# GNN layer with a ternary feed-forward: a second bank for the block sums, five feed-forward banks, smaller loads

## What is computed

```python
xn = layernorm(x)                                    # 6250 x 512
agg = segment_sum(xn[src], dst); neigh = agg / max(deg, 1)
h = layernorm(xn @ W_self + b_self + neigh @ W_neigh) * gamma + beta
x1 = x + where(h >= 0, h, alpha * h) + xn
z = layernorm(x1)
out = x1 + (silu(z @ Qg.T) * (z @ Qu.T)) @ Qd.T      # Q: ternary weights, one scale per 128 inputs
```

## Time and profile before

| | us |
|---|---|
| runs, median of 3 (lowest to highest) | 1532.24 (1531.26 to 1532.78) |
| the profiled execution | 1530.48 |
| its span, first to last instruction | 1528.0 |
| TensorE busy | 1477.2 (97%) |
| ScalarE busy | 1175.0 (77%) |
| VectorE busy | 1050.5 (69%) |
| GpSimd busy | 941.5 (62%) |

### The profile page before, as it was taken

How to read it: one execution, slowest core, us unless ns; L and a number is a source line. 1 busy time by engine, 2 the same in 40 slices (tenths; PEclk the granted TensorE clock), 3 DMA queues, 4 the chain that set the end, 5 groups by cost and what they waited for, 6 DMA issues and landing times.

```text
span 1528.0 us, 21758 instructions
## 1 busy us (share of the span) xinstructions
PE 1477.2 (97%) x6421; PEld 763.3 (50%) x6422; DVE 1050.5 (69%) x2305; ACT 1175.0 (77%) x2248; POOL 941.5 (62%) x936
## 2 busy tenths in 40 slices
PE   7899998998999999999999999999999998999897
PEld 3444444555555555555555555555555554554343
DVE  8999644566767676675675757667577675765876
ACT  5467720014888888889898897979989998998896
POOL 2113237776777777777777777777777777774000
PEclk9999999999999999999999999999999999999999
DMA  8978459999988888898888878888888888885101
GB/s 309 282 262 260 136 178 336 333 301 279 245 241 250 238 266 248 243 269 215 283 229 253 234 239 246 239 252 233 243 223 245 233 257 242 231 245 145 36 14 41
DMA packets 210386, 353.39 MB, mean 231 GB/s; under 512 B 104986, under 2 KB 104986, under 8 KB 210258
## 3 DMA queue, kind: packets, MB, share of 16 engines
q0 software_dynamic: 70560, 231.27, 52.0%
q1 hardware_dynamic: 139708, 120.73, 26.4%
HBM read 295.79 MB, written 39.62 MB: 220 GB/s over the span
## 4 chain that ended last, share of the span: by engine, by line
PE 84%; DMA 5%; DVE 3%; POOL 3%; issue 2%; SPq 1%; ACT 1%; POOLq 0%; DVEq 0%; ACTq 0%
PE f_ps L971 22%; PE f_ps L972 21%; PE f_ps L785 16%; PE agg_ps L867 11%; PE agg_ps L869 11%; POOL rows L737 3%; PE side_ps L912 1%; DMA x1T<-hsx 1%; DMA rows<-node_table,idx 1%; DMA node_table<-hsx 1%; DMA own_rows<-acc 1%; PE agg_ps L781 1%; DVE st6p L1140 1%; DMA xj<-xnt_rows 1%; PE side_ps L781 1%
## 5 line engine op out<-in xcount | busy, mean ns | idle before, releaser
L737 POOL DMA_INDIRECT rows<-node_table,idx x882 | 893.1, 1013 | 302.5 <-issue 266.0
L1065 ACT ACTIVATE f_ps<-f_ps,ratio 128x512 f32<-128x512 f32 (+2 forms) x1303 | 777.0, 674 | 120.4 <-PE f_ps L972 115.5
L971 PE MATMUL f_ps<-x1T,tern 128*128 128x512 f16 (+2 forms) x1144 | 415.5, 367 | 11.8 <-DMA x1T<-hsx 4.9
L972 PE MATMUL f_ps<-x1T,tern 128*128 128x512 f16 (+2 forms) x1144 | 415.3, 367 | 0.0
L867 PE MATMUL agg_ps<-rows,hot 128*128 128x512 f16 x846 | 323.0, 382 | 7.9 <-DMA rows<-node_table,idx 5.5
L869 PE MATMUL agg_ps<-rows,hot 128*128 128x512 f16 x846 | 320.6, 379 | 0.0
L1415 DVE SCALAR_TENSOR_TENSOR acc<-f_ps,scl,acc 128x512 f32<-128x512 f32 (+2 forms) x143 | 102.3, 716 | 176.5 <-PE f_ps L972 116.3
L971 PE MATMUL f_ps<-hT,tern 128*128 128x512 f16 (+2 forms) x572 | 208.5, 367 | 0.4 <-DVE acc L1415 0.2
L972 PE MATMUL f_ps<-hT,tern 128*128 128x512 f16 (+2 forms) x572 | 208.4, 367 | 0.0
L867 PEld LDWEIGHTS agg_ps<-rows,hot 128*128 128x128 f16 x846 | 119.4, 141 | 115.2 <-issue 35.2
L972 PEld LDWEIGHTS f_ps<-x1T,tern 128*128 128x128 f16 x1144 | 112.1, 98 | 124.7 <-issue 1.8
(11 more groups left out here) (174 smaller groups left out, 1698.9 us busy)
## 6 DMA issues: line engine op xcount, KB each, us to landing
rows<-node_table,idx POOLq DMA_INDIRECT x882
hsx<-own_rows SPq DMA_DIRECT2D x49, 256.0 KB
hsx<-in_x SPq DMA_DIRECT2D x48, 256.0 KB
out_nodes<-work SPq DMA_DIRECT2D x48, 256.0 KB, 3.8
node_table<-work SPq DMA_DIRECT2D x30, 256.0 KB, 2.3
xj<-xnt_rows SPq DMA_DIRECT2D x26, 256.0 KB, 4.5
acc<-own_rows SPq DMA_DIRECT2D x23, 256.0 KB, 4.8
own_rows<-acc SPq DMA_DIRECT2D x23, 256.0 KB, 5.8
```

The costliest lines, as they stand in the source:

```text
L737: pool.indirect_dma_start(out=rows[:, j, :], out_offset=None, in_=table[:, :], in_offset=bass.IndirectOffsetOnAxis(ap=of[:, j:j + 1], axis ...
L971: pe.matmul(to, lhs, parts[0], start=g == 0, stop=False, skip_group_check=True)
L972: pe.matmul(to, lhs, parts[1], start=False, stop=True, skip_group_check=True).then_inc(p_ff, 1)
L1065: act.activation(ps, ps, ACT.Copy, scale=ratio[:, w if up else 2, j:j + 1]).then_inc(a_scaled, 1)
```

## The change

It has six parts.

1. The sums of blocks alternate between `agg_ps` and a new bank `agg2_ps` at all blocks; `sum_step` waits for the read of the block before the last only.
2. `AGG_AT`: one sum step in each of the 18 ticks, in place of none in ticks 0 and 1 and two in ticks 2 and 10.
3. `LANES` 5 in place of 6; the planner gives another order. In the table stage `agg2_ps` is the sixth of the y ring.
4. `HELD_IN` [6, 5, 4, 4, 4] in place of [5, 5, 5, 4, 4]: the sixth held product stands within slot 0.
5. x from block 21 on is loaded block by block, from iteration 2 of the table stage (19 blocks ahead), in place of seven blocks at a time; w_gate comes in three pieces, the second at iteration 0 and the third at 2; w_up in six.
6. gamma, beta and alpha are loaded at iteration 30, the bias at 32, W_self in four parts at 34 to 37.

```diff
--- before.py
+++ after.py
@@ -71,7 +71,7 @@
     LATER = [b for b in range(BLOCKS) if b not in NTH_HELD]
     NTH_LATER = {b: n for n, b in enumerate(LATER)}
     LATER_AT = [3, 6, 9, 12]
-    HELD_IN = [5, 5, 5, 4, 4]
+    HELD_IN = [6, 5, 4, 4, 4]
     HELD_FIRST = 5
     assert sum(HELD_IN) == HELD and HELD_BLOCKS[0] >= len(HELD_IN) + 2
 
@@ -87,7 +87,7 @@
 
 
 
-    LANES = 6
+    LANES = 5
     FROM_LANES = 5
 
     GROUPS_OF = {"up": KT, "down": FT, "own": KT, "out": 1}
@@ -156,7 +156,7 @@
     SLOT_OF = {s: t for (t, k), steps in AT.items() for s in steps}
     AGG_AT = [[] for _ in range(TICKS)]
     for j in range(STEPS):
-        AGG_AT[2 + j * (TICKS - 2) // STEPS].append(j)
+        AGG_AT[j].append(j)
 
 
     def is_last(kind, g):
@@ -220,6 +220,8 @@
 
 
     RANGES_FROM = 9
+
+    LOAD_AHEAD = 19
     TILE_AT, TURN_TILE_AT = {}, {}
     per_block = [0, 0] + [1] * 7 + [0] * 10 + [1] * 21 + [0, 0] + [1] * 5
     assert sum(per_block) == 3 * FT, sum(per_block)
@@ -231,7 +233,8 @@
             n += 1
     TILE_BLOCK = {n: at for at, tiles in TILE_AT.items() for n in tiles}
 
-    PIECES = [(0, 0, 16), (0, 16, NG), (1, 0, 24), (1, 24, NG)] + [(2, FT * i, FT * i + FT) for i in range(KT)]
+    PIECES = [(0, 0, 16), (0, 16, 28), (0, 28, NG)] + [(1, lo, min(lo + 8, NG)) for lo in range(0, NG, 8)] + [
+        (2, FT * i, FT * i + FT) for i in range(KT)]
     PIECE_AT = {}
     for q, (w, lo, hi) in enumerate(PIECES):
         if w:
@@ -316,7 +319,7 @@
         idx_o = sb("idx_o", [P, STEPS], I32)
         dstv_o = sb("dstv_o", [P, STEPS], F32)
 
-        agg_ps, side_ps = bank("agg_ps"), bank("side_ps")
+        agg_ps, agg2_ps, side_ps = bank("agg_ps"), bank("agg2_ps"), bank("side_ps")
         f_ps = [bank(f"f_ps{i}") for i in range(LANES)]
 
 
@@ -356,9 +359,9 @@
         dst_i = hotflat[0:EP, EROW:2 * EROW].bitcast(I32)
         tern32 = tern[:, :, :, :].rearrange("p w g k -> p w (g k)").bitcast(F32)
         hit = [tern32[0:EP, w, 0:BLOCKS * NSEG].rearrange("p (b s) -> p b s", b=BLOCKS) for w in (1, 2)]
-        YB = LANES
         own_ps = f_ps[LANES - 1]
-        t_ps, y_ps = [agg_ps, side_ps], f_ps
+        t_ps, y_ps = [agg_ps, side_ps], f_ps + [agg2_ps]
+        YB = len(y_ps)
 
 
         h, t2, neg, x1s = work[:, 0], work[:, 1], work[:, 2], work[:, 3]
@@ -423,7 +426,7 @@
 
         def sums(b):
 
-            return f_ps[0] if b < EARLY and b % 2 else agg_ps
+            return agg2_ps if b % 2 else agg_ps
 
         def held_bank(d):
             return f_ps[(2 + d) % 4] if d < HELD_FIRST else f_ps[2 + d % 2]
@@ -448,11 +451,13 @@
         def _(sp):
             def load_x(g):
                 lo, hi = LOADED[g]
-                hi = min(hi, BLOCKS - 1)
                 buf = xgroup[(lo // GROUP) % 3][:, lo % GROUP:lo % GROUP + hi - lo]
-                if lo >= 3 * GROUP:
-                    sp.wait_ge(a_xn, lo - 2 * GROUP)
                 sp.dma_start(buf, x[lo * P:hi * P, :].rearrange("(t p) d -> p t d", p=P)).then_inc(ld_x[g], 16)
+
+            def load_block(b):
+
+                sp.wait_ge(a_xn, b - 3 * GROUP + 1)
+                sp.dma_start(xb(b), x[b * P:(b + 1) * P, :]).then_inc(ld_x[b // GROUP + 3], 16)
 
             by_tile = [w.rearrange("(i p) (g k) -> p i g k", p=P, k=P) for w in (w_gate, w_up, w_down)]
 
@@ -486,8 +491,8 @@
 
             def load_once(i):
 
-                if i == 0:
-                    load_piece(1)
+                if i in (0, 2):
+                    load_piece(1 + i // 2)
                 if i == 1:
                     load_x(5)
                 if i == 3:
@@ -499,15 +504,16 @@
                         ld_pads, 16)
                     sp.dma_start(src_pad[E:E + PASS].rearrange("(p e) -> p e", p=P), padi[:, :]).then_inc(ld_pads, 16)
                     sp.dma_start(dst_pad[E:E + PASS].rearrange("(p e) -> p e", p=P), padf[:, :]).then_inc(ld_pads, 16)
-                if i == 5:
+                if i == 30:
                     sp.dma_start(gamma_b[:, :], gamma.rearrange("(a d) -> a d", a=1).broadcast_to((P, D))).then_inc(ld_const, 16)
                     sp.dma_start(beta_b[:, :], beta.rearrange("(a d) -> a d", a=1).broadcast_to((P, D))).then_inc(ld_const, 16)
                     sp.dma_start(alpha_c[:, :], alpha.rearrange("(a d) -> a d", a=1).broadcast_to((P, 1))).then_inc(ld_const, 16)
-                if i == 6:
+                if i == 32:
                     sp.dma_start(own_rows[BIAS:BIAS + P, :], b_self.rearrange("(a d) -> a d", a=1).broadcast_to((P, D))).then_inc(
                         st_bias, 16)
-                if i == 8:
-                    sp.dma_start(wself[:, :, :], W_self.rearrange("(k p) n -> p k n", p=P)).then_inc(ld_self, 16)
+                if 34 <= i < 34 + KT:
+                    k = i - 34
+                    sp.dma_start(wself[:, k], W_self[k * P:(k + 1) * P, :]).then_inc(ld_self, 16)
                 if i == BLOCKS - 5:
                     sp.wait_ge(ld_pads, 64)
                     sp.wait_ge(v_rngi, 1)
@@ -535,8 +541,8 @@
 
             for i in range(BLOCKS):
                 load_once(i)
-                if i % GROUP == 5 and i // GROUP + 3 < GROUPS:
-                    load_x(i // GROUP + 6)
+                if 3 * GROUP <= i + LOAD_AHEAD < BLOCKS - 1:
+                    load_block(i + LOAD_AHEAD)
                 for q in PIECE_AT.get(i, ()):
                     load_piece(q)
                 if i == RANGES_FROM + 2:
@@ -859,9 +865,10 @@
                 if j == 0:
                     pe.wait_ge(v_hot, b + 1)
 
-                    after(pe, v_h0, b - 1 if b < EARLY else b)
+                    after(pe, v_h0, b - 1)
                     if b == 1:
-                        pe.wait_ge(v_hsd, HELD_FIRST)
+                        pe.wait_ge(a_yhi, BLOCKS)
+                        pe.wait_ge(v_ylo, BLOCKS)
                 if j % PER_LOAD == 0:
                     pe.wait_ge(gathered[j // PER_LOAD], (b + 1) * 16 * PER_LOAD)
                 pe.matmul(agg[:, :], hot[:, b % 2, :, j], rows[:, j, 0:D], start=(j == 0), stop=False,
@@ -875,7 +882,7 @@
                 if k == 0:
                     if d < KT:
 
-                        n = max(i for i in range(BLOCKS) if f_ps[i % YB] is held_bank(d))
+                        n = max(i for i in range(BLOCKS) if y_ps[i % YB] is held_bank(d))
                         pe.wait_ge(a_yhi, n + 1)
                         pe.wait_ge(v_ylo, n + 1)
 
@@ -932,7 +939,6 @@
                 elif (c, kind, i, w) not in BEFORE:
 
                     pe.wait_ge(v_hsd, HELD)
-                    pe.wait_ge(v_h0, EARLY)
                     if bank_of == LANES - 1:
                         pe.wait_ge(v_own, FROM_LANES)
                 else:
@@ -972,7 +978,7 @@
                 pe.matmul(to, lhs, parts[1], start=False, stop=True, skip_group_check=True).then_inc(p_ff, 1)
 
             pe.wait_ge(v_scl, 1)
-            pe.wait_ge(ld_self, 16)
+            pe.wait_ge(ld_self, 16 * KT)
             for t in range(SLOTS):
                 for d, k in HELD_AT.get((t, -1), ()):
                     held_part(d, k)
@@ -1298,10 +1304,12 @@
             for i in range(BLOCKS):
                 upto = min(i + 11, GROUP + 2 * (i + 1), BLOCKS)
                 for b in range(done, upto):
-                    if b % GROUP == 0:
-                        dve.wait_ge(ld_x[b // GROUP + 3], 16)
                     if b == BLOCKS - 1:
                         dve.wait_ge(ld_xlast, 16)
+                    elif b >= 3 * GROUP:
+                        dve.wait_ge(ld_x[b // GROUP + 3], 16 * (b % GROUP + 1))
+                    elif b % GROUP == 0:
+                        dve.wait_ge(ld_x[b // GROUP + 3], 16)
                     block_stats(b)
                     if b % GROUP == GROUP - 1:
                         group_scales(b - GROUP + 1, b + 1)
```

## The result

The changed kernel takes 1537.22 us in the median of 16 runs (1531.85 to 1547.81), the kernel before beside it 1532.20 (16 runs): ratio 1.0035, interval 1.0022 to 1.0048 (ratios are of the means). I forecast 1523.8, in 1517.5 to 1532.5, with a chance of 0.08 for slower. It is slower. Its profiled execution took 1536.89 us, with a span of 1534.4.

What follows compares the result with a forecast made beforehand. TensorE, busy 97% of the span, was taken as the bound, so time could come only from its idle stretches. The terms summed to -8.4 us, from a median of 1532.2 to 1523.8, range 1517.5 to 1532.5.

Steps and rivals of the forecast that it cites:

- Table stage, -3.3: Table stage: smaller, later loads shorten TensorE's stall on a table store, limited by VectorE's scales; -3.3 us (0 to -6.2).
- The rival of another wait in the stall's place: Table stage: another wait, on SyncE's queue or VectorE, replaces the stall, so its gain is lost; 1527.1 us, chance 0.12.
- Block 0, -3.4: Blocks 0 and 1: a product moved from block 2 fills waits for gathers; -3.4 us (-2.5 to -3.5).
- Block starts, -3.5: Block starts: a second sum bank removes seven waits for VectorE's read, restarts included; -3.5 us (0 to -3.5).
- Block 5, -0.6: Block 5: the 1.64 us wait for VectorE's read goes, but the next product waits for xj; -0.6 us (0 to -1.8).
- block 7, -0.9: Block 7: the 1.0 us wait at 412.66, one on gathers, goes; -0.9 us (0 to -1.1).
- chunk 10 -3.0: Before chunk 10: TensorE work after the transpose's issue grows from 3.0 to 6.0 us, cutting its wait; -3.0 us (-2 to -5.1).
- chunk 12 +2.5: Before chunk 12: TensorE work after the transpose's issue falls from 4.7 to 1.7 us, adding a wait; +2.5 us (0 to +3.0).
- chunk 3 +0.4: Before chunk 3: TensorE work after the transpose's issue falls from 8.6 to 4.3 us; +0.4 us (0 to +2.4).
- chunks 1 and 11, taken as 0: Before the other chunks: TensorE work after the transpose's issue grows or stays within 0.5 us, so no cost was listed.
- Ring, +3.4: Feed-forward: five banks make releases late; +1.5 in chunk 0, +0.3 in 1 to 10, +1.5 and +0.1 in 11 and 12.
- The slower rival: Chunks 2 to 10: the shorter ring also bites there, nine chunks losing 5 us; 1539.3 us, chance 0.08.

Runs made afterwards that it cites:

- consts_late: The kernel before with part 6 alone (later constants), x and weights loaded as before: 1528.64 us, ratio 0.9981.
- lanes_only: The kernel before with five lanes and the planner's other order (part 3) alone, freed bank only in the y ring: 1541.12 us, ratio 1.0053.
- low_early: The changed kernel with VectorE's low half of x1 at tick 8 instead of 10: 1717.40 us in a group of 1720, ratio 0.9978.
- five_again: The changed kernel with part 5 taken back and the planner's numbers 34 for 35 and 20.2 for 19.2: 1531.22 us, ratio 0.9991.
- six_again: The kernel before with part 6, the sixth held product in slot 0 and 34 for 35 in the planner: 1525.25 us, ratio 0.9957.
- x_blocks: The kernel before with part 6 and x loaded block by block, weight pieces as before: 1717.71 us in a group of 1719, ratio 1.0000.
- loads_only: The kernel before with parts 5 and 6 alone (x by blocks, weight pieces, later constants): 1535.43 us, ratio 1.0011.
- held_back: The changed kernel with five held products again in slot 0 (HELD_IN 5, 5, 5, 4, 4): 1540.86 us, ratio 1.0045.

## Why the prediction was wrong

The profiled spans differ by +6.4 where the sum said -8.4, 14.8 us apart. Step by step:

- **Table stage, -3.3: measured +2.2.** The step that failed is the sentence that SyncE gains little and that VectorE's gap may widen by 0.9. It widened from 1.12 to 5.64 (1.35 + 4.29). I had followed the table stores and not the tiles' transposes in the same queue, although I had written that VectorE has no room until 93; and I had counted the added issues (0.9), not that an issue itself takes longer (3.27 instead of 1.33) nor that a landing does. The gain was real and came from part 6 (-3.3, consts_late); x by blocks moved 0.9; the pieces on top took it away (+4.0 to +6.1). The rival of another wait in the stall's place was the right one, but I had let it cost nothing more than the gain.
- **Block 0, -3.4: right within the traces' spread.** 2.9 by the traces with and without it, 3.3 with six lanes; from before to after 2.0, once block 5's wait is taken off the 3.8.
- **Block starts, -3.5: the size was right (4.0), the cause half right.** The seven waits went, but lanes_only, with one bank, lost only 1.9 there: the order had taken the other 2.1. I had given the second bank all of it.
- **Block 5, -0.6, and block 7, -0.9: 2.3 and 0.3.** The wait of 1.64 went and no wait for xj took its place; at block 7, 0.67 is left of 1.01.
- **Order, chunk 10 -3.0 and chunk 12 +2.5: near in size** (4.93 to 1.78, and none to 3.08, 3.2 with its restart).
- **Order, chunk 3 +0.4: 2.6 with its restart; chunks 1 and 11, taken as 0: 1.3 each.** The failed step took the landing of the transposes as it was before and moved only TensorE's work. The order also decides when VectorE reaches the low half, and the second transpose is issued behind that: at chunk 3 4.11 us after the first instead of 1.25, at chunk 11 2.81 instead of 1.50, at chunk 1 3.25 instead of 2.33. With the low half earlier it is 1.3 at every chunk (low_early).
- **Ring, +3.4: about +5.1** by the waits on releases: 2.1 in chunk 0, 1.7 in 1 to 10, 1.3 behind the sums, where I had 1.5, 0.3 and 1.6. The slower rival, a ring that bites by 5 us in chunks 2 to 10, did not come.
- A turn-back of the output at 1412 waits 0.6 longer, which I had not listed.

Put together: 5.5 in the table stage, 5.3 before chunks (2.2 at 3, 2.6 at 1 and 11, 0.7 at 12, -0.2 at 10), 1.7 on the ring, 0.6 for the turn-back and -0.2 for block 0, the block starts and blocks 5 and 7 together, 12.9 of the 14.8. That these last four add up to the forecast is partly luck, since their errors of +1.4, -0.5, -1.7 and +0.6 cancel. Most of the price of the bank given up was wrong: with the same loads, five lanes and two banks (five_again, 1531.2) are 6.0 us slower than six lanes and one (six_again, 1525.3); the two also differ in the ticks of the sums (part 2) and in 20.2 against 19.2.

Open: how these 6.0 divide between the ring, the low half's place and the wait of 5.41 for xj, whose load took 10.2 us to land against 5.9 in six_again; why issues and landings get longer with parts 5 and 6; and whether the pieces cost by size or by place.

## What to carry to other kernels

When one queue issues every DMA by hand-written order, follow each thing that waits in it, and not only the one the change is meant for: a load put in for store A delays transpose B, and the engine with no room left turns that into the new stall. Add up the issues that move, but expect that they get longer too. When a planner's order moves, recompute the arrival of an operand too, since every in-order engine that makes it walks the same order. And a gain ahead of a stretch that waits for gathers is best filled with work (the sixth product); in consts_late's trace it was waited away, and the clock went with it. Run parts one on top of another as well as alone: the pieces cost 1 to 2.4 us alone, by one wait, and 4 to 6 beside the rest, mostly by another.

## What the runs showed of the hardware

- In two groups the kernel before took 1719 and 1720 us; the kernels' table stages and tails in them took as long as elsewhere. GpSimd's waits in x_blocks there:

```profile
POOL rows L742 <- issue: 252.0, 756, 15.2
POOL rows L742 <- remote: 119.7, 66, 3.8
POOL rows L742 <- PE agg_ps L874: 108.8, 57, 6.1
```

  In consts_late the middle row doesn't exist and the last is 35.7. So gathers are held by something that the profile only calls remote; what it is stays open. In the first of these groups the five-lane kernel with two banks was the fastest, 0.9890 against 0.9965 for the six lanes (elsewhere 0.9991 against 0.9957): which of the two designs is better depends on this state. It is not a matter of the chip alone, as far as the numbers in the record go: the chips are 11 and 0, and chip 0 is also that of loads_only, where the kernel before took 1533.36 us.
- Runs of one kernel spread with the mean granted clock: the changed kernel took 1531.85 us at 0.997 and 1547.81 at 0.991. Within kernels, over 229 runs in the groups of 1532, 0.001 of clock goes with 1.1 us, so that a single profile can't be held against a median to better than about 3 us.
- The clock fell behind a wait of 4.1 us and stretches of little work (consts_late, 0.55 from 245 to 250), and not behind the 3.33 of the earlier trace rows. But the same wait of 3.1 us before chunk 12 was followed by 1.00 in the changed kernel's trace and by 0.66 in held_back's, so the wait before it does not settle it, and it is worth 3 us between two traces.
- SyncE's issue of one transposing DMA took 1.33 us in the kernel before and 3.27 in the changed one (36.22, 36.18); the issue of a 9 KB store (`dst_pad`) took 4.48 and 4.61.
